# Decoder layer on one Trainium2 core: cross-attention scores, and the maxima of two batches, as pairs of products on 64 rows

## What is computed

```python
x = x + attn(layernorm(x))            # 16 heads of 64, causal, softmax over the query axis
x = x + xattn(layernorm(x), ctx, ctx) # 16 heads of 8, softmax over 256 keys
x = x + ffn(layernorm(x))             # 8 experts 128 -> 512 -> 128, the best two weighted

# xattn, B = 4, S = 256, 16 heads with D_K = 8
scores = einsum('bhqd,bhkd->bhqk', Q, K) / sqrt(8)
attn = softmax(scores, axis=-1)
out = einsum('bhqk,bhkd->bhqd', attn, V)
```

## Time and profile before

| | us |
|---|---|
| median of three runs | 326.13 |
| lowest, highest | 325.91, 326.90 |
| the profiled execution's own time | 326.34 |
| its span, first to last instruction | 324.6 |
| TensorE busy, share of the span | 92% |
| VectorE busy | 64% |
| ScalarE busy | 59% |

### The profile page before, as it was taken

How to read it: one execution, slowest core, us unless ns; L and a number is a source line. 1 busy time by engine, 2 the same in 40 slices (tenths; PEclk the granted TensorE clock), 3 DMA queues, 4 the chain that set the end, 5 groups by cost and what they waited for, 6 DMA issues and landing times.

```text
span 324.6 us, 5407 instructions
## 1 busy us (share of the span) xinstructions
PE 297.8 (92%) x1869; PEld 210.2 (65%) x1869; DVE 206.5 (64%) x444; ACT 193.0 (59%) x525; POOL 97.8 (30%) x140
## 2 busy tenths in 40 slices
PE   6789999999989899797989788889999999999995
PEld 2578677877777568453745343436778878678883
DVE  3767657375548885966376673536686867666652
ACT  1569858387747664466276668867655465354451
POOL 7990190035020200720056152055558110000000
PEclk9799999999999999999999999979999999999999
DMA  8900015530100010001084491000000000100001
GB/s 234 210 3 3 1 23 65 67 43 16 36 0 2 16 35 2 5 0 45 5 253 141 112 280 55 3 0 2 0 1 2 0 0 0 35 0 0 2 1 32
DMA packets 14889, 14.06 MB, mean 43 GB/s; under 512 B 2620, under 2 KB 10892, under 8 KB 14860
## 3 DMA queue, kind: packets, MB, share of 16 engines
q1 hardware_dynamic: 13278, 12.92, 16.4%
q10 hardware_dynamic: 1584, 0.80, 0.9%
HBM read 9.94 MB, written 0.52 MB: 32 GB/s over the span
## 4 chain that ended last, share of the span: by engine, by line
PE 73%; DVE 13%; ACT 3%; DMA 3%; issue 3%; SPq 2%; POOL 1%; DVEq 0%; ACTq 0%; POOLq 0%
PE ps L663 7%; PE ps L665 7%; PE ps L664 7%; PE ps L737 6%; PE ps L770 5%; PE ps L782 4%; PE ps L944 4%; PE ps L945 4%; PE ps L946 4%; DVE mneg L1306 4%; PE ps L815 3%; PE ps L852 3%; PE ps L744 2%; SPq L412 2%; DMA w_in<-in_L_attn_W_qkv 2%
## 5 line engine op out<-in xcount | busy, mean ns | idle before, releaser
L1062 ACT ACTIVATE p<-ps,negmax 128x256 f32<-128x256 f32 (+1 forms) x128 | 52.7, 426 | 25.2 <-DVE negmax L1277 24.7
L1392 DVE SCALAR_TENSOR_TENSOR hid_lo<-ps,hid_hi 128x512 fp32r<-128x512 f32 x64 | 43.6, 688 | 33.7 <-ACT hid_hi L1126 33.4
L1306 DVE TENSOR_REDUCE mneg<-ps 128x2 f32<-128x512 f32 x64 | 42.5, 684 | 18.6 <-PE ps L815 18.5
L1126 ACT ACTIVATE hid_hi<-ps 128x512 fp32r<-128x512 f32 x64 | 37.5, 598 | 26.8 <-PE ps L665 26.7
L1092 ACT ACTIVATE px<-ps 128x512 f32<-128x512 f32 x64 | 36.1, 598 | 17.8 <-PE ps L837 17.5
L1277 DVE TENSOR_REDUCE negmax<-ps 128x2 f32<-128x512 f32 (+1 forms) x48 | 32.9, 686 | 19.6 <-PE ps L739 12.5
L815 PE MATMUL ps<-k_st,q_mem 128*128 128x256 bf16 x128 | 24.7, 276 | 9.0 <-DVE mneg L1306 7.6
L504 POOL TENSOR_SCALAR tmp<-mv 128x2 f32<-128x2 f32 x8 | 1.9, 233 | 95.3 <-DVE mv L1301 95.3
L1048 ACT CAST t_hi<-ps 128x512 fp32r<-128x512 f32 x32 | 18.8, 592 | 19.5 <-PE ps L665 18.6
L663 PE MATMUL ps<-x_hi,w_hi 128*128 128x512 f32 x64 | 25.6, 400 | 1.7 <-issue 1.5
L1062 ACT ACTIVATION_READ_ACCUMULATOR p<-ps,negmax 128x1 f32 x128 | 26.6, 208 | 0.0
(11 more groups left out here) (184 smaller groups left out, 663.7 us busy)
## 6 DMA issues: line engine op xcount, KB each, us to landing
w_raw<-in_L_ffn_W SPq DMA_DIRECT2D x2, 1024.0 KB, 6.1
w_last<-in_L_ffn_W SPq DMA_DIRECT2D x8, 256.0 KB, 6.1
k_st<-k_part SPq DMA_DIRECT2D x12, 128.0 KB
q_mem<-q_part SPq DMA_DIRECT2D x48, 32.0 KB
w_in<-in_L_attn_W_qkv ACTq DMA_DIRECT2D x2, 384.0 KB, 6.3
w_in<-in_L_attn_W_qkv SPq DMA_DIRECT2D x2, 384.0 KB, 7.1
resid<-in_x SPq DMA_DIRECT2D x2, 256.0 KB, 4.0
p<-in_L_attn_W_o SPq DMA_DIRECT2D x1, 512.0 KB, 8.3
```

Source lines behind the costliest of these rows:

```text
L1062: last = act.activation(dst, bank[:, n * i:n * i + n], ACT.Exp, bias=negmax[:, kt, h:h + 1], accum_out=psums[:, kt, h:h + 1])
L1126: act.activation(hid[0][:, c, :], ps[:, hidden_banks[NC * k + c], :], ACT.Relu).then_inc(s_ha, 1)
L1306: dve.tensor_reduce(mneg[:, qt, :].rearrange("p (r g) -> p r g", r=2)[:, :, g], ps[:, max_bank[("MX", b, u)], :].rearrange("p (h k) -> p h ...
L1392: dve.scalar_tensor_tensor(hid[1][:, c, :], ps[:, hidden_banks[NC * k + c], :], 0.0, hid[0][:, c, :].bitcast(F32), ALU.max, ALU.subtract). ...
```

## The change

The score products of a group become four: for each block of 128 keys, one product for each head, over the 64 rows that hold this head, 256 columns wide. Each head has its own bank (key block kt in columns 256*kt), and `px` and its reader are laid out to match. All four are issued where CS(.,0) stood; before them TensorE waits for both banks. In batches 2 and 3 the maxima are issued in the same way, two units at a time: four products over 64 rows, each head in its own bank (5 and 6), after a wait for both banks. Their place is right after the group's score products, ahead of the tail units of g-0.5. The counts in MAXIMA are made even. In the last batch groups 0 to 3 use three score banks.

```diff
@@ -44,6 +44,7 @@
 LAST = D - 1
 LOW = 32
 LAST_RING = 3
+PAIRED = 2
 TWO_ONES = 1.0 + 0x3F80 / 2.0 ** 23
 SCALE_X = float(DH) ** -0.5
 
@@ -217,8 +218,8 @@
 
         MAXIMA = (((2, 5), (1, 1, 1, 2, 2, 1, 1), (3, 0), (1, 1, 2, 2, 1), (3, 5)),
                   ((3, 5), (1, 2, 1, 2, 2, 1, 1), (B, 0), (2, 2, 2), (B, 4)),
-                  ((B, 3), (1, 2, 2, 2, 2), (B + 1, 0), (1, 2, 2, 2), (B + 1, 4)),
-                  ((B + 1, 5), (2, 3, 3), (B + 2, 0), (3, 3, 1, 1), (B + 2, 5)))
+                  ((B, 3), (2, 2, 2, 2, 2), (B + 1, 0), (2, 2, 2), (B + 1, 4)),
+                  ((B + 1, 5), (2, 2, 2), (B + 2, 0), (4, 2, 2, 2), (B + 2, 5)))
 
 
 
@@ -280,14 +281,20 @@
                     (3, 3): [("WT", 0), ("WS", 0, 3)], (3, 4): [("X", 0)]}
             for g in range(HP):
                 maxima_now, turn = max_plan.get((B + b, g), ([], []))
-                slot = [("CS", b, g, 0)] + tail.get(g - 0.5, []) + more.get((b, g - 0.5), []) + maxima_now[:1] + [("CS", b, g, 1)]
+                paired = maxima_now[:2] if maxima_now and maxima_now[0][1] >= PAIRED else []
+                maxima_now = maxima_now[len(paired):]
+                slot = [("CS", b, g, 0)] + paired + tail.get(g - 0.5, []) + more.get((b, g - 0.5), [])
+                slot += (maxima_now[:1] if not paired else []) + [("CS", b, g, 1)]
                 if b == 0:
                     slot += tail.get(g, [])
                 if g in (2, 4, 6):
                     slot += [("CO", b, g // 2 - 1)]
                 if g == 0 and b >= 1:
                     slot += [("CO", b - 1, 3)]
-                slot += maxima_now[1:2] + turn + (tail.get(g, []) if b else []) + maxima_now[2:] + more.get((b, g), [])
+                if paired:
+                    slot += maxima_now + turn + (tail.get(g, []) if b else []) + more.get((b, g), [])
+                else:
+                    slot += maxima_now[1:2] + turn + (tail.get(g, []) if b else []) + maxima_now[2:] + more.get((b, g), [])
                 if (b, g) < (last, 6):
                     slots.append(slot)
 
@@ -325,7 +332,7 @@
 
         def score_bank(b, k):
 
-            return k % 3 if b < B - 1 else k % 2
+            return k % 3 if b < B - 1 or k < 2 * (HP * (B - 1) + 4) else k % 2
 
         def out_bank(m):
             return 3 + m % 2 if m < 2 * B - 1 else 3
@@ -810,6 +817,20 @@
                         pe.wait_ge(s_vx_ev, 1)
                 if ("MX", b, u) == first_in_5:
                     pe.wait_ge(s_z_ev, 4 * B)
+                if b >= PAIRED:
+
+                    if u % 2 == 0:
+                        for n in range(2):
+                            ge(pe, s_mx_ev, max_before[("MX", b, u + n)])
+                        for i in range(TPB):
+                            for par in range(2):
+                                r = slice(64 * par, 64 * par + 64)
+                                last = pe.matmul(ps[:, max_bank[("MX", b, u + par)], S * i:S * i + S],
+                                                 q_st[b][r, g, S * par + P * i:S * par + P * i + P],
+                                                 k_st[r, g, S * b:S * b + S], start=(i == 0), stop=(i == TPB - 1))
+                                if i == TPB - 1:
+                                    last.then_inc(s_mx, 1)
+                    return
                 ge(pe, s_mx_ev, max_before[("MX", b, u)])
                 for par in range(2):
                     last = pe.matmul(ps[:, max_bank[("MX", b, u)], S * par:S * par + S],
@@ -825,17 +846,24 @@
                                      ident_b[:, :], start=True, stop=True)
                 last.then_inc(s_misc, 1)
 
-            def cross_scores(b, g, kt):
-
-                if g == 0 and kt == 0:
+            def cross_scores(b, g):
+
+                if g == 0:
                     pe.wait_ge(s_mst[b], 16 * 2)
-                k = 2 * (HP * b + g) + kt
-                if k < 3:
-                    pe.wait_ge(s_exp, 12 * B - 2 + k)
-                else:
-                    pe.wait_ge(s_px, last_in(score_banks[k], enumerate(score_banks[:k])) + 1)
-                pe.matmul(ps[:, score_banks[k], :], k_st[:, g, S * b + P * kt:S * b + P * kt + P], q_st[b][:, g, :],
-                          start=True, stop=True).then_inc(s_st, 1)
+                k = 2 * (HP * b + g)
+                for n in (k, k + 1):
+                    if n < 3:
+                        pe.wait_ge(s_exp, 12 * B - 2 + n)
+                    else:
+                        pe.wait_ge(s_px, last_in(score_banks[n], enumerate(score_banks[:n])) + 1)
+                for kt in range(TPB):
+                    for par in range(2):
+                        r = slice(64 * par, 64 * par + 64)
+                        last = pe.matmul(ps[:, score_banks[k + par], S * kt:S * kt + S],
+                                         k_st[r, g, S * b + P * kt:S * b + P * kt + P],
+                                         q_st[b][r, g, S * par:S * par + S], start=(kt == 0), stop=(kt == TPB - 1))
+                        if kt == TPB - 1:
+                            last.then_inc(s_st, 1)
 
             def cross_out(b, g4):
 
@@ -848,7 +876,7 @@
                 for kt in range(2):
                     for j in range(4):
                         h = 2 * g4 + j // 2 + 8 * (j % 2)
-                        p = px[:, g4 % 2, 1024 * (j // 2) + 512 * kt + S * (j % 2):][:, 0:S]
+                        p = px[:, g4 % 2, 1024 * (j // 2) + 512 * (j % 2) + S * kt:][:, 0:S]
                         last = pe.matmul(ps[32 * j:32 * j + 32, out_bank(m), S * (g4 % 2):S * (g4 % 2) + S],
                                          v_pad[:, TPB * b + kt, (DH + 1) * h:(DH + 1) * h + 32], p, start=(kt == 0), stop=(kt == 1))
                 last.then_inc(s_pv, 1)
@@ -973,7 +1001,8 @@
                     elif kind == "mT":
                         max_turn(b)
                     elif kind == "CS":
-                        cross_scores(b, *i)
+                        if i[1] == 0:
+                            cross_scores(b, i[0])
                     elif kind == "CO":
                         cross_out(b, *i)
                     elif kind in ("oq0", "oT0", "oq1", "oT1", "wo"):
@@ -1084,11 +1113,11 @@
                     act.wait_ge(s_misc, misc_at[("PJ", b - 1)] + 1)
                 act.copy(zT[:, 2 * i:2 * i + 2, :], ps[:, ring_bank[("Z", b, i)], :]).then_inc(s_z_ev, 1)
 
-            def cross_probabilities(b, g, kt):
-                k = 2 * (HP * b + g) + kt
+            def cross_probabilities(b, g, par):
+                k = 2 * (HP * b + g) + par
                 act.wait_ge(s_st, k + 1)
                 ge(act, s_pv, 4 * b + g // 2 - 1)
-                c0 = 1024 * (g % 2) + 512 * kt
+                c0 = 1024 * (g % 2) + 512 * par
                 act.activation(px[:, (g // 2) % 2, c0:c0 + 512], ps[:, score_banks[k], :], ACT.Exp,
                                scale=SCALE_X).then_inc(s_px, 1)
 
@@ -1303,7 +1332,8 @@
             def cross_max(b, u):
                 g, qt = u // 2, u % 2
                 dve.wait_ge(s_mx, 16 * b + u + 1)
-                dve.tensor_reduce(mneg[:, qt, :].rearrange("p (r g) -> p r g", r=2)[:, :, g],
+                by_head = mneg[:, :, :].rearrange("p t (r g) -> p t r g", r=2)[:, :, :, g]
+                dve.tensor_reduce(by_head[:, :, qt] if b >= PAIRED else by_head[:, qt, :],
                                   ps[:, max_bank[("MX", b, u)], :].rearrange("p (h k) -> p h k", h=2), AX, ALU.max,
                                   negate=True).then_inc(s_mx_ev, 1)
 
```

## The result

The changed kernel is slower: 331.44 us in the median of six runs (328.12 to 332.45) against 325.19 (324.04 to 326.90) for the kernel before; ratio 1.0175, 95% interval 1.012 to 1.023, about 5.7 us (the medians are 6.25 us apart). The direction was forecast, the size (+0.95 us) and the range (up to 329.0) were not. The profiled execution took 332.45 us with a span of 330.7.

A forecast was written before the change was run, and what follows sets the result against it. Three successive chains (q to batch 3's first maxima, VectorE's maxima to batch 1's residual, GpSimd's norm to the gates) were taken as the bound; 0 + 0.3 + 0.9 - 0.35 - 0.2 + 0.3 = +0.95 us on 326.13 gave 327.1, range 324.0 to 329.0.

The forecast's parts named there:

- Pairs and tiles: TensorE's score and maxima products: pairs on 64 rows overlap wholly, 0.21 us a foursome; a block's tile changes cost 0.2 us.
- a group of scores alone gains nothing: Groups without maxima: the 0.21 us saved by pairing is offset by 0.2 us for changing tiles.
- Up to PJ: Batch 0 until PJ of batch 3: shorter scores gain some 0.6 us, then given back; 0, ends -0.3 and +0.3.
- The new wait: Slot (0,3), ahead of PJ: the second of two maxima needs bank 5, still being reduced; gives back the 0.6 us.
- n2T and q: Last batch, after PJ: both stand behind pairs of maxima, q starts near 168.75 instead of 168.45; +0.3, ends 0 and +0.8.
- Maxima of batch 3: VectorE's maxima and batch 1's residual: waiting for both banks opens gaps between pairs; +0.9, ends +0.2 and +2.0.
- Four gaps: Between batch 3's eight pairs of maxima: four of seven gaps uncovered by other VectorE work, 0.48 each, 1.9 us.
- Gates: WT to X and a little before: shorter scores and a shared switch save time; -0.35, ends -0.7 and 0.
- The third bank: Last batch's scores ahead of the gates: removes a TensorE wait for ScalarE, but WT waits for VectorE; 0.
- Clock: TensorE's granted clock: longer idle stretches lower it; +0.3, ends 0 and +1.75, priced from the fall among the first experts.
- one more fall: One more drop of TensorE's clock, on top of the summed terms: 328.6 us; part of a rival with chance 0.17.
- pairs that don't overlap: 64-row products run one after another, 6.6 us of switches without gain: 329.4 us; part of a rival with chance 0.17.

The follow-up runs named there:

- e1: Changed kernel with the maxima of the kernel before; scores still in pairs, three score banks in the last batch: 324.63 us, ratio 0.9994.
- e2: Changed kernel with the scores of the kernel before; maxima of batches 2 and 3 still paired, three score banks: 329.0 us, ratio 1.0128.
- e10: Changed kernel with the score foursome issued twice in seven groups ahead of the two clock falls: 327.60 us, ratio 1.0096.
- e5: Changed kernel with each unit of maxima by itself, over all rows, waiting for one bank; places and counts kept: 325.63 us, ratio 1.0017.
- e4: Changed kernel with the tail units of g-0.5 ahead of the paired maxima again: 327.34 us, ratio 1.0067.
- e12: Kernel with paired scores, old maxima and q of the last batch early, set back from three score banks to two: 324.58 us, ratio 0.9994.
- e11: Kernel before with only q of the last batch moved ahead of the seventh group's scores: 323.32 us, ratio 0.9947.

## Why the prediction was wrong in its size

- **Pairs and tiles.** Right: 0.23 us a foursome, near 0.1 us a change of tiles. That a group of scores alone gains nothing held for the whole: e1 is at 0.9994.
- **Up to PJ.** Priced at 0; 0.15 us late. The new wait was there: scores alone bring PJ 0.6 us forward, the changed kernel gives it back. With the old scores and the paired maxima (e2) PJ is 0.94 us late.
- **n2T and q.** Priced at +0.3, ends 0 and +0.8. It was 0.9 without any clock fall (e2; 0.7 in e10), because the second and third pair each waited for the reduction of the one before, and 2.1 in the changed kernel. The mechanism was right, the term too small.
- **Maxima of batch 3.** Priced at +0.9, ends +0.2 and +2.0; measured 1.27, and 1.57 against the same order without the wait for both banks (e5). Four gaps were open, as counted; each was 0.56 us, not 0.48.
- **Gates.** Priced at -0.35; e1, e4 and e5 show 0. The shorter scores save nothing between NT and X. The third bank, priced at 0, hides 0.5 us that the wait for both score banks would otherwise cost (e12); this wait I had not priced at all.
- **Clock.** This is the step that failed. "I add +0.3, with 0 and +1.75 (one more fall like this) as ends": there were two more falls, both on a chain that sets the end, 1.4 and 2.2 us by the marks against e10, together more than twice the upper end of the term. I had taken the price from a fall that hardly hurts: among the first experts it costs 0.6 us (X to X(2) 11.6 with it, 11.03 without). Where TensorE's products are the chain itself a fall costs more: the CO of 1.07 us took 1.94. I had also tied the fall to the idle 1.52 us ahead of it, and e11 has this wait without a fall. The Trainium skill ("TensorE: Matmul & The Clock Gate", Why this matters for your kernels) names idle gaps between bursts as what brings the half rate back. This case agrees in the direction only: the changed kernel's waits ahead of the two falls were 0.35 to 1.08 us with work between, and e11's wait of 1.52 us brought none.
- **Chances.** 0.43 stood on slower, but the two ways to lose more, pairs that don't overlap and one more fall, had been put together at 0.17, the first of them (329.4) outside the range. Two more falls on the chains were in no rival.

The account is an estimate from kernels that were measured at different times, each beside runs of the kernel before: the wait for both banks 2.0 us by the medians (327.60 less 325.63) or 2.6 by the ratios (e10 against e5, whose mean clocks are alike), the clock 3.8 or 2.6 us (changed against e10), the rest of the change 0.4 to 0.6 us, which can't be told from nothing. What is open: why the falls come just there. In 176 to 200 us the changed kernel has TensorE busy less (5.2 to 5.5 of each 8 us) and its clock is full; from run to run the number of falls differs. The redundant products also shift the work behind them in time, and no run here tells that apart from the added work.

## What to carry to other kernels

An order that lets two products go side by side is paid for where both destinations must be free at once: two banks used in turn hide the producer behind the reader, two banks used together do not. Before taking work from an engine that is busy 92% of the time, see what it waits for in the stretch, and count what the idle time does to TensorE's clock on the chains that set the end; seven redundant groups of products were worth 2.6 to 3.8 us here. The cheap gain lay in the place of one unit at the head of a long chain (0.5%).

## What was not expected of the hardware

More work on TensorE made the kernel faster: the changed kernel is at 331.44 us, with 1.5 us of redundant products 327.60, with 6.9 us 328.61, and with all products over 128 rows 328.32. And the granted clock differs between runs of one program: six runs of the changed kernel spread over 4.3 us, with mean clocks from 0.969 to 0.990. A wait of 1.52 us ahead of the first expert is followed by a fall in one kernel (before) and by none in another (e11).
